# Local attention in a six-layer block on one core: probability transposes moved behind the output product, directly ahead of the next scores

## The chip, the cores and the metric

One core of a Trainium2 chip. The metric is the device time of one execution in microseconds; lower is better. Engines: TensorE (PE) with its weight loads (PEld), VectorE (DVE), ScalarE (ACT), GpSimd (POOL), and SyncE (SP), which issues DMAs.

## The reference, cut to what matters

Input is `x`, (2, 1024, 128), f32. A first small attention with 16 heads of 8 columns and two layer norms comes first, and a layer norm last. In between stand six layers, which take most of the time:

```python
for i in range(6):
    x = attn_layer(shift_tokens(x), Wqkv[i], q_scale[i], k_scale[i], Wo[i]) + x
    x = ffn_layer(shift_tokens(x), ln_g[i], ln_b[i], W1[i], b1[i], W2[i], b2[i]) + x

# attn_layer: 16 heads of 64, windows of 32
q, k, v = split(x @ Wqkv)
q, k = l2norm(q) * qs, l2norm(k) * ksc
q, k = rotary(q), rotary(k)                      # cos, sin and a scale per position
attn = softmax(mask(q @ k.T * 8))                # each row sees itself and the 32 keys before it
out  = (attn @ v) @ Wo
```

`shift_tokens` moves the upper half of the columns by one row.

## The kernel before, in words

It is written in Bass, with a program for each engine and hand-placed semaphores: each engine runs its own list in order, and waits on counters that the others raise. Rows come in 16 tiles of 128. In a layer, `layer` on each engine runs `tiles(...)`, which calls `tile(t, n, p, opening, closing)` for each of the 16 tiles (first and last two written out, the others in a loop of two; `opening` is the first, `closing` the last), and then the feed-forward part in four groups of four tiles. The order of work around the change is thus the order of calls in the `tile` of each engine.

A tile is software-pipelined. While the scores and products of tile t run, the projections of tile t+1 are made, and what is left of tile t-1 is finished:

- `project(t+1, ., x)`, x = 0 to 5 (L1180 to L1182): six blocks of 512 columns of q, k and v in two PSUM banks, three matmuls each. Blocks 0, 1, 2, 4 are q and k, blocks 3 and 5 are v.
- ScalarE: `square` (L494) of a q or k block, `values` (L501) evacuates a v block.
- VectorE: `rotary(t+1, ., j)`, j = 0 to 3: norms (L791, `n` is `n2`), `tc_` (L794), `n2c` (L798), `ts_` (two of L801). It waits for the square.
- GpSimd: `rotate`: a power (L317), a sum (L319), a product into `w_nat` (L322); four times a tile.
- TensorE: `transpose_heads(., j, at)` (L1187) of `w_nat`; ScalarE: `heads_T` (L516) evacuates it to `qT` or `kT`.
- TensorE: `scores(t, n, p, G)`, G = 0 and 1, eight heads each: mask (L1137) and scores (L1146) into the two banks SB.
- VectorE: `maxima(t, p, G)`, two reductions (L748). ScalarE: `exps(t, p, G, b)`, b = 0 and 1, four exponentials each (L478).
- TensorE: `transpose_probs(t, G, b, at)` (L1153). ScalarE: `probs_out` (L487) evacuates to `pT`.
- TensorE: `weigh_values(t, p, G)` (L1166), probabilities by values. VectorE: `heads_out(t, p, G)`, reciprocal (L756) and product into `o_nat` (L758).
- TensorE: `transpose_out(t, G, at)` (L1193). ScalarE: `heads_out_T` (L507) to `oT`. TensorE: `project_out(t, G)` (L1201) with `Wo`. VectorE: `residual` (L765, L766) adds the input.
- `copy_prev` (VectorE, L773) carries the last 32 keys into the next tile; `copy_input` (ScalarE, L426, L427) and `input_rest` (VectorE, L780) prepare the input of tile t+2 in two parts.

The transposes share a ring of two PSUM banks, bank 4 and bank 6, which the last argument of each call (`at`) names. Each use waits until the bank's last content is evacuated; the counters `tp_free` (heads), `pt_evac` (probabilities) and `ot_evac` (outputs) tell that. So whoever moves a transpose also changes what its neighbours wait for. In the last tile of a layer the layer norm of the feed-forward part is interleaved: `transpose_in`, `norm_stats`, `norm`, `transpose_normed`, `normed_T`.

In the order before, the two `transpose_probs` of a group stand three or four steps behind its scores, with two projections, a transpose of heads and a product with the values in between.

Of the kernel before, what the change touches and what calls it, by code (L numbers as in the profile page):

```python
# [6 lines left out]
TILES = B * N // P  # L7
# [38 lines left out]
def build(nc, x, Wa, ba, Wp, bp, Wqkv, Wo, scales, W1, W2, par, rope, ident, identb, mask, mask_l, select, out):  # L46
# [3 lines left out]
    with ctx:  # L50
# [351 lines left out]
        def _(eng):  # L402
# [167 lines left out]
            def layer(l, last):  # L570
                t0 = l * TILES

                def tile(t, n, p, opening, closing):
                    if closing:
                        shifted(l, 0)
                        shifted(l, 1)
                    exps(t, p, 0, 0)
                    if not closing:
                        square(t + 1, 0)
                    heads_T(t, p, 2, 6 if opening else 4)  # L580
                    exps(t, p, 0, 1)
                    if not closing:
                        square(t + 1, 1)
                    probs_out(t, 0, 0, 4 if opening else 6)
                    probs_out(t, 0, 1, 6 if opening else 4)
                    if not opening:
                        heads_out_T(t - 1, 1, 6)
                    if not closing:
                        square(t + 1, 2)
                    heads_T(t, p, 3, 4)  # L590
                    exps(t, p, 1, 0)
                    if closing:
                        normed_T(0)
                    else:
                        values(t + 1, 1 - p, 0)
                        heads_T(t + 1, 1 - p, 0, 6)
                    exps(t, p, 1, 1)
                    if not closing and not (isinstance(n, int) and n == TILES - 2):
                        copy_input(n + 2, p)
                    probs_out(t, 1, 0, 4)  # L600
                    probs_out(t, 1, 1, 6)
                    if not closing:
                        square(t + 1, 3)
                    heads_out_T(t, 0, 4)
                    if closing:
                        normed_T(1)
                    else:
                        values(t + 1, 1 - p, 1)
                        heads_T(t + 1, 1 - p, 1, 6)

# [63 lines left out]
        def _(eng):  # L674
# [202 lines left out]
            def layer(l, last):  # L877
# [45 lines left out]
                def tile(t, n, p, opening, closing):  # L923
# [7 lines left out]
                    if closing:  # L931
                        norm(0)
                    else:
                        rotary(t + 1, n + 1, 1)
                    if not opening:
                        residual(t - 1, n - 1)
                    if closing:
                        norm_stats(1)
                    else:
                        copy_prev(t + 1, n + 1, 1 - p)  # L940
                    maxima(t, p, 1)
                    if closing:
                        norm(1)
                    else:
                        rotary(t + 1, n + 1, 2)
                    heads_out(t, p, 0)
                    if not closing:
                        if not (isinstance(n, int) and n == TILES - 2):
                            input_rest(t + 2, n + 2, p)
                        rotary(t + 1, n + 1, 3)  # L950
# [62 lines left out]
        def _(eng):  # L1013
# [230 lines left out]
            def layer(l, last):  # L1244
# [42 lines left out]
                def tile(t, n, p, opening, closing):  # L1287
# [6 lines left out]
                    else:  # L1294
                        project(t + 1, 1 - p, 0)
                    if opening:
                        eng.wait_ge(tp_free, t * 4 + 1)
                    else:
                        eng.wait_ge(ot_evac, t * 2 - 1)
# [5 lines left out]
                    if not opening:  # L1305
                        weigh_values(t - 1, 1 - p, 1)
                    eng.wait_ge(tp_free, t * 4 + 2)
                    transpose_probs(t, 0, 0, 4 if opening else 6)
                    eng.wait_ge(tp_free, t * 4 + 3)
                    transpose_probs(t, 0, 1, 6 if opening else 4)  # L1310
                    if not opening:
                        eng.wait_ge(pt_evac, t * 4 + 1)
# [3 lines left out]
                    eng.wait_ge(pt_evac, t * 4 + (1 if opening else 2))  # L1316
                    transpose_heads(t, 3, 4)
                    if not opening:
                        project_out(t - 1, 1)
                    scores(t, n, p, 1)  # L1320
                    if not closing:
                        project(t + 1, 1 - p, 3)
                    if opening:
                        eng.wait_ge(pt_evac, t * 4 + 2)
                    else:
                        eng.wait_ge(ot_evac, t * 2)
# [4 lines left out]
                    weigh_values(t, p, 0)  # L1331
                    eng.wait_ge(tp_free, t * 4 + 4)
                    transpose_probs(t, 1, 0, 4)
                    if closing:
                        eng.wait_ge(f_xnT, l * SUPERS + 1)
                    else:
                        eng.wait_ge(tp_free, t * 4 + 5)
                    transpose_probs(t, 1, 1, 6)
                    if not closing:
                        project(t + 1, 1 - p, 4)  # L1340
                    eng.wait_ge(pt_evac, t * 4 + 3)
                    transpose_out(t, 0, 4)
                    if not closing:
                        project(t + 1, 1 - p, 5)
                    eng.wait_ge(pt_evac, t * 4 + 4)
                    if closing:
                        transpose_normed(1)
                    else:
                        transpose_heads(t + 1, 1, 6)
                    project_out(t, 0)  # L1350

                def close_layer(t, n, p):
                    gate_up(0, 0)
                    weigh_values(t, p, 1)
                    eng.wait_ge(ot_evac, t * 2 + 1)
# [101 lines left out]
```

## Time and profile before

| what | value |
|---|---|
| median of 3 runs | 2512.28 us (2510.72 to 2596.46) |
| profiled execution | 2513.5 us, its span 2511.7 us |
| TensorE busy in the span | 2084.1 us |
| VectorE, ScalarE, GpSimd busy | 1743.5, 1632.6, 1740.9 us |
| mean granted TensorE clock | 0.966 of full |

The span is that of the profile's own records; the profiled execution's time is 1.8 us above it. "Idle before" in brackets is the time that an engine stood still right before an instruction, with the one that ended it. PE busy counts matmuls with their pipelined ends. In a timeline, instructions of one line that follow each other are one row, and its second column runs to the end of the last.

### The profile page before, as it was taken

How to read it: one execution, taken by the hardware profiler on the slowest of the kernel's cores; microseconds unless marked ns; L12 is line 12 of the kernel's file. 1: busy time of each engine (PE TensorE's matmuls, PEld its weight loads, DVE VectorE, ACT ScalarE, POOL GpSimd, SP SyncE). 2: the span in 40 equal slices, each digit the busy share in tenths (PEclk: the TensorE clock that was granted, in tenths of full speed). 3: DMA queues.
4: the chain of work that ended last, by engine and by line, in shares of the span. 5: the costliest groups of instructions: out<-in, count | busy, mean ns of one | idle time of the engine just before them, and what ended most of it. 6: DMA issues, size and time to landing. Idle time of an engine off the chain costs nothing.

```text
span 2511.7 us, 70965 instructions
## 1 busy us (share of the span) xinstructions
PE 2084.1 (83%) x23552; PEld 1533.5 (61%) x23552; DVE 1743.5 (69%) x4197; ACT 1632.6 (65%) x5654; POOL 1740.9 (69%) x1364
## 2 busy tenths in 40 slices
PE   6999478888888888888888888888788888888886
PEld 4666356666566666466666466665466665566663
DVE  4555667777667777577776777775777776777764
ACT  3555257767567777577776577776577775777772
POOL 4333468888578787588885788885788885888860
PEclk9999779999999999999999999999999999999998
DMA  1000111111021111111111121111211110111110
GB/s 61 1 0 0 43 53 49 40 38 38 22 75 40 46 40 39 53 45 38 38 48 33 54 50 40 38 39 34 63 41 47 39 38 22 48 44 44 38 37 17
DMA packets 40902, 98.65 MB, mean 39 GB/s; under 512 B 6480, under 2 KB 20432, under 8 KB 39856
## 3 DMA queue, kind: packets, MB, share of 16 engines
q1 hardware_dynamic: 40752, 96.75, 14.9%
q8 instruction: 82, 1.34, 0.2%
q14 instruction: 68, 0.56, 0.1%
HBM read 20.32 MB, written 1.05 MB: 9 GB/s over the span
## 4 chain that ended last, share of the span: by engine, by line
PE 39%; issue 19%; DVE 17%; ACT 15%; POOL 8%; DVEq 1%; POOLq 0%; ACTq 0%; DMA 0%; SPq 0%
ACT prob L478 10%; PE bank L1201 5%; PE bank L1146 5%; DVE nmax L748 3%; PE bank L1193 3%; PE bank L1187 3%; DVE ts_ L801 3%; PE bank L1137 3%; DVE o_nat L758 2%; PE bank L1180 2%; ACT qT L516 2%; POOL tsum L319 2%; PE bank L1182 2%; PE bank L1181 2%; PE bank L1050 2%
## 5 line engine op out<-in xcount | busy, mean ns | idle before, releaser
L317 POOL TENSOR_TENSOR rn<-n2c,half_neg 128x8 f32<-128x8 f32 x384 | 632.9, 1648 | 351.0 <-DVE n2c L798 341.8
L478 ACT ACTIVATE prob<-bank,nmax 128x96 f32<-128x96 f32 x1536 | 508.7, 360 | 401.9 <-DVE nmax L748 401.7
L319 POOL TENSOR_TENSOR tsum<-tc_,ts_ 128x512 f32<-128x512 f32 x384 | 493.3, 1285 | 0.0
L1153 PE MATMUL bank<-idf,prob 128*96 128x128 f32 x1536 | 247.2, 285 | 241.6 <-ACT prob L478 241.6
L322 POOL TENSOR_TENSOR w_nat<-tsum,rn 128x512 f32<-128x512 f32 x384 | 401.0, 1044 | 37.8 <-POOL tsum L319 15.1
L791 DVE TENSOR_REDUCE n<-nat 128x8 f32<-128x512 f32 x384 | 261.3, 680 | 188.9 <-ACT nat L494 122.3
L478 ACT ACTIVATION_READ_ACCUMULATOR prob<-bank,nmax 128x1 f32 x1536 | 347.0, 226 | 0.0
L1153 PEld LDWEIGHTS bank<-idf,prob 128*96 128x96 f32 x1536 | 152.9, 128 | 301.1 <-issue 288.6
L1180 PE MATMUL bank<-w_hi,xs 128*128 128x512 f32 x576 | 288.9, 502 | 9.5 <-DVE ts_ L801 7.0
L801 DVE TENSOR_TENSOR ts_<-bank,ropeL 128x256 f32<-128x256 f32 x768 | 285.8, 412 | 0.0
L748 DVE TENSOR_REDUCE nmax<-bank 128x4 f32<-128x384 f32 x384 | 196.1, 552 | 125.5 <-PE bank L1146 117.6
L494 ACT ACTIVATE nat<-bank 128x512 f32<-128x512 f32 x384 | 235.5, 613 | 55.7 <-PE bank L1182 54.0
L794 DVE TENSOR_TENSOR tc_<-bank,ropeL 128x512 f32<-128x512 f32 x384 | 261.2, 680 | 0.0
L780 DVE TENSOR_TENSOR xs_lo<-xA,xs 64x128 fp32r<-64x128 f32 x192 | 189.0, 984 | 72.7 <-ACT xs L427 69.5
L1187 PE MATMUL bank<-idf,w_nat 128*128 128x128 f32 x1536 | 233.5, 275 | 4.2 <-POOL w_nat L322 2.8
L1182 PE MATMUL bank<-w_hi,xs_lo 128*128 128x512 f32 x576 | 232.5, 404 | 0.5 <-issue 0.5
L1181 PE MATMUL bank<-w_lo,xs 128*128 128x512 f32 x576 | 232.9, 404 | 0.0
L1187 PEld LDWEIGHTS bank<-idf,w_nat 128*128 128x128 f32 x1536 | 192.8, 141 | 62.7 <-issue 6.9
L1166 PEld LDWEIGHTS bank<-vspace,pT 96*64 96x64 f32 x6144 | 195.0, 138 | 52.5 <-issue 52.5
L1166 PE MATMUL bank<-vspace,pT 96*64 96x64 f32 x6144 | 221.5, 225 | 0.0
L487 ACT ACTIVATE pT<-bank 96x512 f32<-96x512 f32 x384 | 213.1, 608 | 11.2 <-PE bank L1153 9.0
L1201 PE MATMUL bank<-oT,wo 128*128 128x128 f32 x1536 | 209.1, 280 | 4.1 <-ACT oT L507 4.1
(129 smaller groups left out, 3988.1 us busy)
## 6 DMA issues: line engine op xcount, KB each, us to landing
vspace<-v_nat SPq DMA_DIRECT2D x96, 384.0 KB, 4.0
vspace<-v_nat SPq DMA_DIRECT2D x96, 256.0 KB, 3.5
vspace<-v_nat SPq DMA_DIRECT2D x95, 128.0 KB, 2.3
nat<-w_qkv SPq DMA_DIRECT2D x5, 1536.0 KB, 7.8
wo<-w_o SPq DMA_DIRECT2D x6, 512.0 KB, 4.0
w<-w SPq DMA_DIRECT2D x6, 341.0 KB, 3.0
shared<-w_qkv SPq DMA_DIRECT2D x1, 1536.0 KB, 6.6
w<-w SPq DMA_DIRECT2D x6, 192.0 KB, 3.0
```

The source lines that it names most:

```text
L317: nc.gpsimd.tensor_tensor(rn[:, r, :], n2c[:, r, :], half_neg[:, 0:8], ALU.pow).then_inc(pool_step, 1)
L319: nc.gpsimd.tensor_tensor(tsum[:, r, :], tc_[:, r, :], ts_[:, r, :], ALU.add).then_inc(pool_step, 1)
L322: nc.gpsimd.tensor_tensor(w_nat[:, r, :].rearrange("p (h d) -> p h d", d=D), tsum[:, r, :].rearrange("p (h d) -> p h d", d=D), rn[:, r, :] ...
L478: last = nc.scalar.activation(prob[:, 4 * b + i, :], SB[b][:, i * SPAN:(i + 1) * SPAN], ACT.Exp, bias=nmax[:, p, 8 * G + 4 * b + i:8 * G + ...
L801: last = nc.vector.tensor_tensor(ts_[:, r, :].rearrange(heads3, d=D)[:, :, lo:lo + D // 2], pj[:, :].rearrange(heads3, d=D)[:, :, hi:hi + ...
L1153: last = nc.tensor.transpose(RING[at][0:SPAN, i * P:(i + 1) * P], prob[:, 4 * b + i, :], idf[:, :])
L1166: last = nc.tensor.matmul(OB[qs, a:a + D], pT[:, 4 * b + i, qs], vw[:, p, half, head * D:(head + 1) * D], start=True, stop=True, skip_grou ...
L1180: nc.tensor.matmul(PJ[x % 2][:, :], xs[:, p, :], hi, start=True, stop=False)
L1181: nc.tensor.matmul(PJ[x % 2][:, :], xs[:, p, :], rest, start=False, stop=False)
L1182: nc.tensor.matmul(PJ[x % 2][:, :], xs_lo[:, p, :], hi, start=False, stop=True).then_inc(pj_ready, 1)
L1187: last = nc.tensor.transpose(RING[at][:, i * P:(i + 1) * P], w_nat[:, j % 2, i * P:(i + 1) * P], idf[:, :])
L1201: last = nc.tensor.matmul(YB[:, 0:P], wo[:, 4 * G + i, :], oT[:, G, i * P:(i + 1) * P], start=G == 0 and i == 0, stop=G == 1 and i == 3)
```

## The change

Three engines' lists are reordered; no arithmetic is added or taken away, and SyncE and GpSimd are untouched. On TensorE, `weigh_values` of the group before moves up to directly behind the first projection; the two `transpose_probs` of a group move down behind `project_out`, directly ahead of the next group's scores; the bank numbers and waits are changed to fit. ScalarE follows: the second `exps` comes before the copy of heads, and `probs_out` goes to where its transposes now are. On VectorE, `residual` and `copy_prev` move from ahead of the second maxima to behind `rotary(., 2)` and `heads_out`.

```diff
 # ScalarE, tile
                     exps(t, p, 0, 0)
                     if not closing:
                         square(t + 1, 0)
+                    exps(t, p, 0, 1)
                     heads_T(t, p, 2, 6 if opening else 4)
-                    exps(t, p, 0, 1)
                     if not closing:
                         square(t + 1, 1)
-                    probs_out(t, 0, 0, 4 if opening else 6)
-                    probs_out(t, 0, 1, 6 if opening else 4)
                     if not opening:
                         heads_out_T(t - 1, 1, 6)
                     if not closing:
                         square(t + 1, 2)
                     heads_T(t, p, 3, 4)
+                    probs_out(t, 0, 0, 6)
+                    probs_out(t, 0, 1, 4)
                     exps(t, p, 1, 0)
...
                         values(t + 1, 1 - p, 0)
+                    exps(t, p, 1, 1)
+                    if not closing:
                         heads_T(t + 1, 1 - p, 0, 6)
-                    exps(t, p, 1, 1)
...
                         heads_T(t + 1, 1 - p, 1, 6)
+                    probs_out(t, 1, 0, 4)
+                    probs_out(t, 1, 1, 6)
 # VectorE, tile
                     if closing:
                         norm(0)
+                        norm_stats(1)
                     else:
                         rotary(t + 1, n + 1, 1)
-                    if not opening:
-                        residual(t - 1, n - 1)
-                    if closing:
-                        norm_stats(1)
-                    else:
-                        copy_prev(t + 1, n + 1, 1 - p)
                     maxima(t, p, 1)
                     if closing:
                         norm(1)
                     else:
                         rotary(t + 1, n + 1, 2)
+                    if not opening:
+                        residual(t - 1, n - 1)
                     heads_out(t, p, 0)
                     if not closing:
+                        copy_prev(t + 1, n + 1, 1 - p)
                         if not (isinstance(n, int) and n == TILES - 2):
                             input_rest(t + 2, n + 2, p)
                         rotary(t + 1, n + 1, 3)
 # TensorE, tile
                         project(t + 1, 1 - p, 0)
+                    if not opening:
+                        weigh_values(t - 1, 1 - p, 1)
                     if opening:
                         eng.wait_ge(tp_free, t * 4 + 1)
                     else:
-                        eng.wait_ge(ot_evac, t * 2 - 1)
+                        eng.wait_ge(pt_evac, t * 4 - 1)
                     transpose_heads(t, 2, 6 if opening else 4)
...
                         project(t + 1, 1 - p, 1)
                     if not opening:
-                        weigh_values(t - 1, 1 - p, 1)
-                    eng.wait_ge(tp_free, t * 4 + 2)
-                    transpose_probs(t, 0, 0, 4 if opening else 6)
-                    eng.wait_ge(tp_free, t * 4 + 3)
-                    transpose_probs(t, 0, 1, 6 if opening else 4)
-                    if not opening:
-                        eng.wait_ge(pt_evac, t * 4 + 1)
+                        eng.wait_ge(pt_evac, t * 4)
                         transpose_out(t - 1, 1, 6)
                     if not closing:
                         project(t + 1, 1 - p, 2)
-                    eng.wait_ge(pt_evac, t * 4 + (1 if opening else 2))
+                    eng.wait_ge(tp_free, t * 4 + (2 if opening else 3))
                     transpose_heads(t, 3, 4)
                     if not opening:
                         project_out(t - 1, 1)
+                    if opening:
+                        eng.wait_ge(tp_free, t * 4 + 3)
+                    else:
+                        eng.wait_ge(ot_evac, t * 2)
+                    transpose_probs(t, 0, 0, 6)
+                    eng.wait_ge(tp_free, t * 4 + 4)
+                    transpose_probs(t, 0, 1, 4)
+
                     scores(t, n, p, 1)
                     if not closing:
                         project(t + 1, 1 - p, 3)
...
+                    weigh_values(t, p, 0)
+                    eng.wait_ge(pt_evac, t * 4 + 1)
                     if closing:
                         transpose_normed(0)
                     else:
                         transpose_heads(t + 1, 0, 6)
-                    weigh_values(t, p, 0)
-                    eng.wait_ge(tp_free, t * 4 + 4)
+                        project(t + 1, 1 - p, 4)
+                    eng.wait_ge(pt_evac, t * 4 + 2)
+                    transpose_out(t, 0, 4)
+                    if closing:
+                        eng.wait_ge(f_xnT, l * SUPERS + 1)
+                        transpose_normed(1)
+                    else:
+                        project(t + 1, 1 - p, 5)
+                        eng.wait_ge(tp_free, t * 4 + 5)
+                        transpose_heads(t + 1, 1, 6)
+                    project_out(t, 0)
+                    eng.wait_ge(ot_evac, t * 2 + 1)
                     transpose_probs(t, 1, 0, 4)
...
                     transpose_probs(t, 1, 1, 6)
-                    if not closing:
-                        project(t + 1, 1 - p, 4)
-                    eng.wait_ge(pt_evac, t * 4 + 3)
-                    transpose_out(t, 0, 4)
...
-                    project_out(t, 0)
```

The instruction lists show the same. On TensorE, in the half tile between scores(t, ., ., 0) and scores(t, ., ., 1) of a layer's second tile, behind the scores and project 0, the kernel before has:

```order
L1187 MATMUL bank<-idf,w_nat 128x128 x4
L1180 MATMUL bank<-w_hi,xs 128x512
L1181 MATMUL bank<-w_lo,xs 128x512
L1182 MATMUL bank<-w_hi,xs_lo 128x512
L1166 MATMUL bank<-vspace,pT 64x64 x16
L1153 MATMUL bank<-idf,prob 96x128 x8
L1193 MATMUL bank<-idf,o_nat 128x128 x4
L1180 MATMUL bank<-w_hi,xs 128x512
L1181 MATMUL bank<-w_lo,xs 128x512
L1182 MATMUL bank<-w_hi,xs_lo 128x512
L1187 MATMUL bank<-idf,w_nat 128x128 x4
L1201 MATMUL bank<-oT,wo 128x128 x4
```

In the changed kernel (its TensorE lines are two lower, so L1151 is the probability transpose) TensorE has at the same place:

```order
L1164 MATMUL bank<-vspace,pT 64x64 x16
L1185 MATMUL bank<-idf,w_nat 128x128 x4
L1178 MATMUL bank<-w_hi,xs 128x512
L1179 MATMUL bank<-w_lo,xs 128x512
L1180 MATMUL bank<-w_hi,xs_lo 128x512
L1191 MATMUL bank<-idf,o_nat 128x128 x4
L1178 MATMUL bank<-w_hi,xs 128x512
L1179 MATMUL bank<-w_lo,xs 128x512
L1180 MATMUL bank<-w_hi,xs_lo 128x512
L1185 MATMUL bank<-idf,w_nat 128x128 x4
L1199 MATMUL bank<-oT,wo 128x128 x4
L1151 MATMUL bank<-idf,prob 96x128 x8
```

The product with the values went from behind the second projection to ahead of the heads' transposes, and the eight probability transposes from ahead of the output transposes to the end of the half. On VectorE, in a layer's third tile, the kernel before has between rotary(., 1) and the end of heads_out(t, 0):

```order
L765 TENSOR_TENSOR xB<-bank,xA 128x1
L766 TENSOR_TENSOR xB<-bank,xA 128x128
L773 TENSOR_SCALAR kT<-kT,follows 128x8x32
L748 TENSOR_REDUCE nmax<-bank 128x4 x2
L791 TENSOR_REDUCE n<-nat 128x8
L794 TENSOR_TENSOR tc_<-bank,ropeL 128x512
L798 TENSOR_SCALAR n2c<-n 128x8
L801 TENSOR_TENSOR ts_<-bank,ropeL 128x8x32 x2
L756 RECIPROCAL linv<-lsum 128x8
L758 TENSOR_TENSOR o_nat<-bank,linv 128x512
```

and the changed kernel:

```order
L748 TENSOR_REDUCE nmax<-bank 128x4 x2
L791 TENSOR_REDUCE n<-nat 128x8
L794 TENSOR_TENSOR tc_<-bank,ropeL 128x512
L798 TENSOR_SCALAR n2c<-n 128x8
L801 TENSOR_TENSOR ts_<-bank,ropeL 128x8x32 x2
L765 TENSOR_TENSOR xB<-bank,xA 128x1
L766 TENSOR_TENSOR xB<-bank,xA 128x128
L756 RECIPROCAL linv<-lsum 128x8
L758 TENSOR_TENSOR o_nat<-bank,linv 128x512
L773 TENSOR_SCALAR kT<-kT,follows 128x8x32
```

The residual (L765, L766) now stands between the rotary and heads_out, and the copy of keys (L773) behind heads_out.

## Rows read from the trace of the kernel before

**Rows 1.** The page: busy time of each engine, TensorE's slices, one group
```profile
PE 2084.1 (83%) x23552; PEld 1533.5 (61%) x23552; DVE 1743.5 (69%) x4197; ACT 1632.6 (65%) x5654; POOL 1740.9 (69%) x1364
...
PE   6999478888888888888888888888788888888886
...
L780 DVE TENSOR_TENSOR xs_lo<-xA,xs 64x128 fp32r<-64x128 f32 x192 | 189.0, 984 | 72.7 <-ACT xs L427 69.5
```

**Rows 2.** Stretch of six tiles: us; PE, PEld, DVE, ACT, POOL busy; clock; DMA
```profile
865.09:980.70 115.61, 97.98 (x1237) 76.56 (x1237) 89.02 (x198) 84.68 (x300) 94.45 (x74) 1.00 0.17 41
```

**Rows 3.** Waits in the same six tiles: total us, times, longest
```profile
POOL rn L317 <- DVE n2c L798: 18.2, 12, 1.6
...
PE bank L1153 <- ACT prob L478: 13.8, 12, 1.5
```

**Rows 4.** Timeline, half A: start us, us, engine, line, [idle before <- releaser]
```profile
913.37 0.50 PE L1137 MATMUL bank<-mskL,idb 128*128 x2
...
914.76 1.02 DVE L748 TENSOR_REDUCE nmax<-bank 128x4 f32<-128x384 f32 x2 [0.77 <-PE bank L1146]
...
916.63 0.61 ACT L494 ACTIVATE nat<-bank 128x512 f32<-128x512 f32 x1
...
917.38 0.69 DVE L791 TENSOR_REDUCE n<-nat 128x8 f32<-128x512 f32 x1 [1.60 <-ACT nat L494]
...
917.73 0.64 PE L1153 MATMUL bank<-idf,prob 128*96 128x128 f32 x4
...
919.16 0.61 PE L1153 MATMUL bank<-idf,prob 128*96 128x128 f32 x4 [0.79 <-ACT prob L478]
919.32 0.19 DVE L756 RECIPROCAL linv<-lsum 128x8 f32<-128x8 f32 x1
...
920.29 0.66 PE L1193 MATMUL bank<-idf,o_nat 128*128 128x128 f32 x4 [0.51 <-DVE o_nat L758]
...
922.91 0.50 PE L1137 MATMUL bank<-mskL,idb 128*128 x2
```

**Rows 5.** Timeline, half B of the tile before it
```profile
903.66 0.50 PE L1137 MATMUL bank<-mskL,idb 128*128 x2
904.00 0.16 DVE L765 TENSOR_TENSOR xB<-bank,xA 128x1 f32 x1 [0.84 <-PE bank L1201]
...
904.41 0.35 DVE L773 TENSOR_SCALAR kT<-kT,follows 128x256 f32<-128x256 f32 x1
...
905.98 0.67 DVE L791 TENSOR_REDUCE n<-nat 128x8 f32<-128x512 f32 x1
...
909.45 0.61 PE L1153 MATMUL bank<-idf,prob 128*96 128x128 f32 x4 [1.48 <-ACT prob L478]
...
909.82 0.48 PE L1180 MATMUL bank<-w_hi,xs 128*128 128x512 f32 x1
```

**Rows 6.** Stretches: first and last of the 7 half tiles with a fallen clock
```profile
366.18:377.58 11.40, 9.69 (x106) 7.72 (x104) 8.84 (x19) 7.54 (x26) 9.24 (x8) 0.85 0.01 1
...
2383.61:2394.93 11.32, 9.69 (x105) 7.78 (x104) 8.84 (x19) 7.60 (x26) 8.93 (x8) 0.85 0.00 0
```

**Rows 7.** Stretches behind the last probability transposes of layers 1, 2 and 6
```profile
644.20:647.80 3.60, 3.35 (x21) 2.25 (x19) 0.00 (x0) 3.21 (x5) 0.00 (x0) 1.00 0.00 0
1006.80:1010.40 3.60, 3.54 (x19) 3.14 (x18) 0.00 (x0) 2.72 (x4) 0.00 (x0) 0.54 0.00 0
...
2447.70:2451.30 3.60, 3.60 (x19) 3.23 (x18) 0.00 (x0) 2.57 (x4) 0.00 (x0) 0.55 0.00 0
```

**Rows 8.** Timelines: last tile of layer 2, first tile of layer 3
```profile
1000.45 0.16 DVE L765 TENSOR_TENSOR xB<-bank,xA 128x1 f32<-128x1 f32 x1 [2.20 <-PE bank L1201]
...
1004.37 0.61 PE L1153 MATMUL bank<-idf,prob 128*96 128x128 f32 x4 [1.14 <-ACT prob L478]
...
1006.33 0.62 PE L1153 MATMUL bank<-idf,prob 128*96 128x128 f32 x4 [1.35 <-ACT prob L478]
...
1065.51 1.06 PE L1153 MATMUL bank<-idf,prob 128*96 128x128 f32 x4 [3.60 <-ACT prob L478]
```

More of the change, by code:

```diff
@@ L595, in tile @@
                         values(t + 1, 1 - p, 0)
+                    exps(t, p, 1, 1)
+                    if not closing:
                         heads_T(t + 1, 1 - p, 0, 6)
-                    exps(t, p, 1, 1)
[L598 to L601, printed above, removed]
-                    if not closing:
+                        if not (isinstance(n, int) and n == TILES - 2):
+                            copy_input(n + 2, p)
                         square(t + 1, 3)
@@ L1322, in tile @@
                         project(t + 1, 1 - p, 3)
[L1323 to L1326, printed above, removed]
+                    weigh_values(t, p, 0)
+                    eng.wait_ge(pt_evac, t * 4 + 1)
                     if closing:
@@ L1330, in tile @@
                         transpose_heads(t + 1, 0, 6)
-                    weigh_values(t, p, 0)
-                    eng.wait_ge(tp_free, t * 4 + 4)
+                        project(t + 1, 1 - p, 4)
[10 more added lines that the diff above has]
+                    eng.wait_ge(ot_evac, t * 2 + 1)
                     transpose_probs(t, 1, 0, 4)
                     if closing:
-                        eng.wait_ge(f_xnT, l * SUPERS + 1)
+                        eng.wait_ge(f_xnT, l * SUPERS + 2)
                     else:
-                        eng.wait_ge(tp_free, t * 4 + 5)
+                        eng.wait_ge(tp_free, t * 4 + 6)
                     transpose_probs(t, 1, 1, 6)
-                    if not closing:
-                        project(t + 1, 1 - p, 4)
-                    eng.wait_ge(pt_evac, t * 4 + 3)
-                    transpose_out(t, 0, 4)
[L1343 to L1349, printed above, removed]
-                    project_out(t, 0)
                 def close_layer(t, n, p):
@@ L1354, in close_layer @@
                     weigh_values(t, p, 1)
-                    eng.wait_ge(ot_evac, t * 2 + 1)
+                    eng.wait_ge(pt_evac, t * 4 + 3)
                     transpose_out(t, 1, 4)
```

## The prediction

> **What bounds the kernel now.** Start with the page. Its busy shares put TensorE at 83% and no other engine above 69% [rows 1]; the 40 slices look alike from the sixth to the last but one, so one repeating piece carries the time. That piece is the attention tile. I looked next at the table of stretches, for six tiles in the middle of layer 2: 115.61 us, or 19.27 per tile, at full clock; TensorE is busy 97.98 of it (16.3 per tile), GpSimd 94.45 (15.7) [rows 2]. No engine is full: about 2.9 us of TensorE per tile are waits, and a tile could not go far under 16.4. The list of waits of the same stretch names them: TensorE before the probability transposes waits 13.8 us in 12 waits for the exponentials; GpSimd waits 18.2 us for `n2c` [rows 3]. So the tile is a loop of dependences that goes through all engines. The two timelines show it. I call the part from scores(t,0) to scores(t,1) half A (it takes 922.91 - 913.37 = 9.54 us [rows 4]) and the part from scores(t,1) to the next tile's scores half B (913.37 - 903.66 = 9.71 [rows 4, 5]).
>
> In half A the path from the scores is: maxima 1.39 us after the scores start, the exponentials, the square of projection 0 at 3.26, VectorE's rotary(0) from 4.01, the reciprocal of heads_out(t-1,1) at 5.95, and the transposes of that output at 6.92, for which TensorE stands still 0.51 us although it also did the probability transposes meanwhile (from 4.36 and from 5.79, after a wait of 0.79) [rows 4]. 2.62 us later the next scores start [rows 4]. In half B the path is scores, maxima, both blocks of exponentials; TensorE waits 1.48 us for the second, and goes on at 5.79 [rows 5].
>
> **The change, part by part.** It adds and removes no arithmetic instruction; it moves some.
>
> (1) *Half A, first part.* The chain scores, maxima, first exponentials, square, rotary(0), heads_out is the same on ScalarE and VectorE in the new order. weigh_values(t-1,1) moves ahead of the transposes of heads 2, and ends early, but VectorE takes heads_out only behind rotary(0), whose square stands behind the first four exponentials. So the output transposes still cannot start before 6.92 us after the scores. What stood in front of them is gone, though: the two blocks of probability transposes now come later. TensorE's remaining work there (scores, project 0, weigh, heads 2, project 1) is what stands in the first 4.36 us of the old half A [rows 4]; so TensorE now idles from about 4.5 to 6.9 us, 2.4 us in one piece, where it had 0.79 and 0.51 in two.
>
> (2) *Half A, second part.* Behind the output transposes come project 2, heads 3, project_out as before (2.62 us to where the scores stood), and now the two blocks of probability transposes, on the path: one block holds TensorE 909.82 - 909.45 = 0.37 us [rows 5], two 0.74. The exponentials are long done, so there is no wait. Half A: 6.92 + 2.62 + 0.74 = 10.28, against 9.54: +0.74.
>
> (3) *Half B.* The probability transposes at its middle are gone, and with them the 1.48 us wait. What is late next is VectorE. In the new order it goes maxima, rotary(2), residual, heads_out(t,0). From the scores to the first instruction of the rotary is 905.98 - 903.66 = 2.32 us [rows 5]; a rotary takes 919.32 - 917.38 = 1.94 us [rows 4]; the residual, moved to this place, 904.41 - 904.00 = 0.41 [rows 5]; from the reciprocal to the output transposes 920.29 - 919.32 = 0.97 [rows 4]. Together 5.64. TensorE has less work than that in front of them (project 3, weigh, heads 0, project 4), so it waits here too, though under 1 us at a time. Then 2.62 + 0.74 = 3.36 as in half A. Half B: 9.00, against 9.71: -0.71.
>
> (4) *The tile.* 10.28 + 9.00 = 19.28, against 19.25. The order by itself gives nothing: the waits for the exponentials are exchanged for waits for heads_out, and the transposes leave the shade of a wait for the path. The sum contains no small gaps; I take +0.1 per tile, bounds -0.1 to +0.4 (the upper one if the copy of keys and the remainder of the input, now behind heads_out on VectorE, push rotary(3) into the next maxima: they took 0.35 us [rows 5] and 2 x 0.98 [rows 1], and there is 3.36 + 1.39 = 4.75 us for them and the rotary's 1.94, so about 0.5 spare). For 84 tiles (14 inner ones in each of 6 layers) that is +8 us, bounds -8 to +34.
>
> (5) *TensorE's clock.* This is what I expect to decide. The trace shows how idle stretches and the granted clock go together. With a single idle stretch of 1.48 us per tile the clock stays at full (2.4 GHz) nearly always: the six tiles above have a granted clock of 1.00 [rows 2]. In 7 half tiles of the whole run it fell to half (1.2 GHz) right behind that wait, mean 0.85 over the half tile; the first and the last of them took 11.40 and 11.32 us where 9.71 is usual: +1.65 [rows 5, 6]. In the last tile of a layer TensorE idles twice within 3 us, 1.14 and 1.35 [rows 8], and behind it the clock is 0.54 in layer 2 and falls like that in five of the six layers (not in the first) [rows 7]. In a layer's first tile an idle stretch of 3.60 us ends with four transposes that take 1.06 us in place of 0.61: half clock [rows 8]. So: 1.5 us, rarely (7 of 84); 2.5 us in two pieces, 5 of 6; 3.6 us, yes. The new 2.4 us stretch in every tile sits next to the second. I take two tiles in three, bounds none and all. What follows the stretch at half clock (output transposes, project 2, heads 3, project_out, probability transposes) is all on the path, so each fall costs its full 1.65 us: 84 x 2/3 x 1.65 = +92 us, bounds 0 and +139. The 7 old falls, 7 x 1.65 = 12 us, come off.
>
> The Trainium skill (TensorE: Matmul & The Clock Gate, section "Why this matters for your kernels") speaks of the same danger but asks only that TensorE-idle gaps between bursts stay below a length that is above my 2.4 us. By that rule no clock would fall here, and the time would be that of the first rival below. The trace disagrees with it as it stands: the clock fell behind waits of 1.48 us.
>
> (6) *Edges of a layer.* First tile: the two blocks of probability transposes used to stand in front of a wait for heads 3 and now follow it: +0.74 x 6 = +4. Last tile: VectorE's residual waited 2.20 us for project_out with the second norm statistics and the maxima queued behind it [rows 8]; they now go ahead of it. I take -1.5 per layer (0 to -2.2 by that row, and something back because transpose_normed(1) now stands ahead of the last probability transposes): -9. Together -5, bounds -12 to +6. SyncE's and GpSimd's orders are untouched; the values' DMA is issued after the same signals, half a tile and more before it is used.
>
> *The sum:* profiled execution 2513.5 (span 2511.7) + 8 + 92 - 12 - 5 = 2596.5; the median of the runs, 2512.3, lies 1.2 below that execution, so 2595.
>
> **The rivals.**
> *A. The clock stands.* The order acts as in (1) to (4) but the 2.4 us stretch does not trip the clock: 2513.5 + 8 - 5 - 1 = 2516 (the old falls kept; without them 2504). For it: the first layer's last tile kept its clock [rows 7], and 77 of 84 waits of 1.5 us did. Against it: the five others.
> *B. Faster: the waits vanish.* If VectorE had heads_out ready when project 1 is done, half A would keep only the +0.74 less its old waits, and half B lose its 1.48: about 19.27 - 1.48 = 17.8 per tile, 84 x -1.48 = -124: 2388. It decides at 4.5 us after the scores; the row has the reciprocal at 5.95 and the transposes at 6.92 [rows 4], and nothing on VectorE's or ScalarE's way there is taken out. At the extreme, all 2.9 us of waits gone, GpSimd (15.7) and TensorE (16.3) would bound the tile.
> *C. VectorE late as well.* The copy of keys and the input remainder are held by GpSimd's additions, rotary(3) ends after the next scores, and the maxima wait: +0.4 per tile on top of falls in nearly every tile: 2513.5 + 34 + 139 - 12 - 5 - 1 = 2668.
>
> **How the numbers follow.** Forecast case 0.65, A 0.23, B 0.04, C 0.08. The forecast case runs from 2558 (two falls in five tiles) to 2642 (a fall in every tile); with A below it the range is 2510 to 2640, which leaves out B, most of C and little else. About 2% (2462 and 2562.5) is what a measurement of this kernel can tell from no change. Slower by more: the forecast case and C, less the low end of the first: 0.70. Within: 0.26. Faster: 0.04.
>
> **What would show it.** In the changed profile: per inner tile, output transposes of heads_out 6.9 us after the first scores behind an idle stretch of about 2.4 us released by `o_nat`; no wait of L1151 (the probability transposes) for the exponentials; half A at 10.3 (11.9 where the clock falls), half B at 9.0; a mean granted clock of about 0.90 to 0.93 in the middle of a layer, where it was 1.00; GpSimd's waits for `n2c` not shorter. I am wrong on (1) if the output transposes come before 6 us; on (5) if the middle of a layer keeps a clock of 1.00; on (3) if TensorE doesn't wait for `o_nat` in half B; on (4) if tiles at full clock take under 18.9 or over 19.7.

## The result and the profile after

The changed kernel takes 2611.9 us (median of 4 runs, 2608.3 to 2698.8), the kernel before beside it 2513.0 (2510.7 to 2596.5). The ratio is 1.038, with a 95% interval of 1.032 to 1.044: slower. (One run of each, the highest, was disturbed and is left out of the ratio.) The forecast was 2595 with a range of 2510 to 2640. The profiled execution took 2608.3 us, its span is 2606.4, its mean granted clock 0.936 (0.966 before).

The page of the changed kernel: busy times (one line) and three groups (line, engine, shapes, count | busy us, mean ns | idle before, releaser). They answer to [rows 1]:

```profile
PE 2165.5 (83%) x23552; PEld 1599.1 (61%) x23552; DVE 1729.8 (66%) x4197; ACT 1645.9 (63%) x5654; POOL 1747.3 (67%) x1364
...
L478 ACT ACTIVATE prob<-bank,nmax 128x96 f32<-128x96 f32 x1536 | 506.7, 355 | 211.5 <-DVE nmax L748 211.3
...
L1178 PE MATMUL bank<-w_hi,xs 128*128 128x512 f32 x576 | 299.9, 521 | 83.1 <-DVE ts_ L801 80.7
L1191 PE MATMUL bank<-idf,o_nat 128*128 128x128 f32 x768 | 147.8, 324 | 235.6 <-DVE o_nat L758 225.1
```

The busy share reads 83% again, and tells nothing: TensorE did the same 23552 matmuls in 81 us more of busy time. The probability transposes no longer wait; the output transposes (L1191) wait 225 us for `o_nat`, and projections 81 us for `ts_`. The page of the kernel before has instead:

```profile
L1153 PE MATMUL bank<-idf,prob 128*96 128x128 f32 x1536 | 247.2, 285 | 241.6 <-ACT prob L478 241.6
```

The timeline of a half A at full clock, in the middle of layer 3, answers to [rows 4] (start us, us, engine, line, [idle before <- releaser]):

```profile
1209.07 0.49 PE L1135 MATMUL bank<-mskL,idb 128*128 x2
...
1210.45 1.02 DVE L748 TENSOR_REDUCE nmax<-bank 128x4 f32<-128x384 f32 x2 [0.43 <-PE bank L1144]
...
1213.15 0.69 DVE L791 TENSOR_REDUCE n<-nat 128x8 f32<-128x512 f32 x1 [1.68 <-ACT nat L494]
...
1215.08 0.19 DVE L756 RECIPROCAL linv<-lsum 128x8 f32<-128x8 f32 x1
...
1216.06 0.66 PE L1191 MATMUL bank<-idf,o_nat 128*128 128x128 f32 x4 [2.41 <-DVE o_nat L758]
...
1218.57 1.04 PE L1151 MATMUL bank<-idf,prob 128*96 128x128 f32 x8
...
1219.44 0.49 PE L1135 MATMUL bank<-mskL,idb 128*128 x2
```

The reciprocal starts 6.01 us after the scores and the output transposes 6.99; before, it was 5.95 and 6.92. TensorE idles 2.41 us in one piece. The eight probability transposes stand at the end, with no wait, and half A is 10.37 us. In the next tile the same half meets half clock. First its rows in the timeline of TensorE, then stretches (us; PE, PEld, DVE, ACT, POOL busy; clock; DMA): the half A above (with the 0.12 us before it), the half B behind it, and this half A.

```profile
1235.51 0.99 PE L1191 MATMUL bank<-idf,o_nat 128*128 128x128 f32 x4 [2.33 <-DVE o_nat L758]
1236.15 0.78 PE L1178 MATMUL bank<-w_hi,xs 128*128 128x512 f32 x1
...
1239.65 1.04 PE L1151 MATMUL bank<-idf,prob 128*96 128x128 f32 x8
```

```profile
1208.95:1219.44 10.49, 8.08 (x106) 6.45 (x105) 7.09 (x18) 7.04 (x25) 8.62 (x7) 1.00 0.29 72
1219.44:1228.60 9.16, 8.51 (x105) 6.44 (x103) 7.69 (x16) 7.28 (x27) 7.23 (x6) 1.00 0.03 7
1228.60:1240.52 11.92, 9.59 (x105) 7.79 (x103) 6.94 (x18) 7.03 (x25) 10.26 (x8) 0.86 0.25 61
```

Behind the 2.33 us the four transposes take 0.99 instead of 0.66 and a projection's first matmul 0.78 instead of 0.48: the granted clock is 0.86 over this half, where it is 1.00 in the other two, so for a part of it the clock was at its lower level of 1.2 GHz. This half takes 11.92.

Half B of the same tile answers to [rows 5]:

```profile
1221.76 0.68 DVE L791 TENSOR_REDUCE n<-nat 128x8 f32<-128x512 f32 x1
...
1223.68 0.15 DVE L765 TENSOR_TENSOR xB<-bank,xA 128x1 f32 x1
...
1223.82 0.51 PE L1178 MATMUL bank<-w_hi,xs 128*128 128x512 f32 x1 [0.50 <-DVE ts_ L801]
1223.94 0.19 DVE L756 RECIPROCAL linv<-lsum 128x8 f32<-128x8 f32 x1
...
1224.17 0.69 DVE L758 TENSOR_TENSOR o_nat<-bank,linv 128x512 f32<-128x512 f32 x1
...
1224.39 0.39 PE L1180 MATMUL bank<-w_hi,xs_lo 128*128 128x512 f32 x1
...
1224.91 0.66 PE L1191 MATMUL bank<-idf,o_nat 128*128 128x128 f32 x4
...
1226.09 0.59 ACT L507 ACTIVATE oT<-bank 128x512 f32<-128x512 f32 x1
...
1226.73 1.16 PE L1199 MATMUL bank<-oT,wo 128*128 128x128 f32 x8
```

The rotary begins at 2.32 after the scores, projection 4 waits 0.50 for it, the output transposes come at 5.47 and project_out at 7.29.

Counting the distances between the starts of the mask matmuls over the 14 inner tiles of each of the six layers gives the account of the inner tiles, in the one profiled execution of each kernel. "Falls" are half tiles of 10.8 us or more; in every kernel these are the same half tiles as those in which the granted clock was under 1.00, and the medians leave them out. The longest wait is that of an inner tile between 1110 and 1340 us.

| kernel | half A, median | half B, median | falls in 84 tiles | mean tile | longest TensorE wait in a tile | run median |
|---|---|---|---|---|---|---|
| before | 9.54 | 9.72 | 7 (B) | 19.39 | 1.5 | 2513.0 |
| changed | 10.32 | 9.16 | 54 (A) | 20.44 | 2.4 | 2611.9 |
| fill6 | 10.32 | 9.15 | 0 | 19.51 | 1.0 | 2529.9 |
| fill2 | 10.32 | 9.15 | 44 (A) | 20.32 | 2.0 | 2599.7 |
| resback | 10.37 | 9.16 | 57 (A) | 20.48 | 2.4 | 2609.8 |
| resci | 10.39 | 8.75 | 63 (A) | 20.44 | 2.4, in most tiles 2.1 | 2607.3 |
| hofirst | 9.28 | 9.66 | 21 (B) | 19.33 | 1.3 | 2512.6 |
| hoffill | 9.29 | 9.67 | 0 | 18.95 | 0.4 | 2477.0 |
| hyb | 9.53 | 9.23 | 0 | 18.79 | 1.0 | 2466.8 |
| hybresci | 9.60 | 9.12 | 0 | 18.84 | 1.0 | 2466.7 |

The rows from fill6 on are the experiments told below. The changed kernel's inner tiles are 84 x (20.44 - 19.39) = 88 us longer in sum than those before. The spans differ by 2606.4 - 2511.7 = 94.7.

### The profile page after: what moved, and what is told of

Read it like the earlier page. It is cut to its first block, busy times and chain, and to the rows that moved or that the text cites. A ratio compares the mean times of both kernels' runs of the same rounds, so it can differ in the third digit from the quotient of the medians.

```text
span 2606.4 us, 71177 instructions
## 1 busy us (share of the span) xinstructions
PE 2165.5 (83%) x23552; PEld 1599.1 (61%) x23552; DVE 1729.8 (66%) x4197; ACT 1645.9 (63%) x5654; POOL 1747.3 (67%) x1364
## 3 DMA queue, kind: packets, MB, share of 16 engines
HBM read 20.32 MB, written 1.05 MB: 8 GB/s over the span
## 4 chain that ended last, share of the span: by engine, by line
PE 47%; DVE 22%; issue 15%; ACT 7%; POOL 7%; DVEq 1%; POOLq 0%; ACTq 0%; DMA 0%; SPq 0%
PE bank L1199 7%; PE bank L1151 6%; PE bank L1144 5%; PE bank L1191 4%; DVE ts_ L801 4%; ACT prob L478 4%; DVE o_nat L758 4%; DVE nmax L748 4%; PE bank L1185 3%; DVE n L791 3%; PE bank L1135 2%; PE bank L1178 2%; ACT nat L494 2%; PE bank L1048 2%; PE bank L1180 2%
## 5 line engine op out<-in xcount | busy, mean ns | idle before, releaser
L322 POOL TENSOR_TENSOR w_nat<-tsum,rn 128x512 f32<-128x512 f32 x384 | 410.6, 1069 | 37.8 <-POOL tsum L319 15.1
L1178 PE MATMUL bank<-w_hi,xs 128*128 128x512 f32 x576 | 299.9, 521 | 83.1 <-DVE ts_ L801 80.7
L1191 PE MATMUL bank<-idf,o_nat 128*128 128x128 f32 x768 | 147.8, 324 | 235.6 <-DVE o_nat L758 225.1
L478 ACT ACTIVATION_READ_ACCUMULATOR prob<-bank,nmax 128x1 f32 x1536 | 339.0, 221 | 0.0
L1191 PEld LDWEIGHTS bank<-idf,o_nat 128*128 128x128 f32 x768 | 94.0, 158 | 313.3 <-DVE o_nat L758 285.0
L1185 PE MATMUL bank<-idf,w_nat 128*128 128x128 f32 x1536 | 266.4, 301 | 6.9 <-ACT qT L516 4.1
L1180 PE MATMUL bank<-w_hi,xs_lo 128*128 128x512 f32 x576 | 242.2, 420 | 0.0
L1179 PE MATMUL bank<-w_lo,xs 128*128 128x512 f32 x576 | 241.4, 419 | 0.4 <-issue 0.4
L1199 PE MATMUL bank<-oT,wo 128*128 128x128 f32 x1536 | 226.9, 294 | 8.7 <-ACT oT L507 6.9
L1199 PEld LDWEIGHTS bank<-oT,wo 128*128 128x128 f32 x1536 | 203.6, 206 | 31.9 <-ACT oT L507 31.4
```

What stands on the lines that cost most here:

```text
L322: nc.gpsimd.tensor_tensor(w_nat[:, r, :].rearrange("p (h d) -> p h d", d=D), tsum[:, r, :].rearrange("p (h d) -> p h d", d=D), rn[:, r, :] ...
L478: last = nc.scalar.activation(prob[:, 4 * b + i, :], SB[b][:, i * SPAN:(i + 1) * SPAN], ACT.Exp, bias=nmax[:, p, 8 * G + 4 * b + i:8 * G + ...
L1178: nc.tensor.matmul(PJ[x % 2][:, :], xs[:, p, :], hi, start=True, stop=False)
L1185: last = nc.tensor.transpose(RING[at][:, i * P:(i + 1) * P], w_nat[:, j % 2, i * P:(i + 1) * P], idf[:, :])
L1191: last = nc.tensor.transpose(RING[at][:, i * P:(i + 1) * P], o_nat[:, G, i * P:(i + 1) * P], idf[:, :])
L1199: last = nc.tensor.matmul(YB[:, 0:P], wo[:, 4 * G + i, :], oT[:, G, i * P:(i + 1) * P], start=G == 0 and i == 0, stop=G == 1 and i == 3)
```

## The experiments

**Filler in the idle stretch.** Is it the clock, or do the waits cost the time and the clock only goes along? The changed kernel gets matmuls into bank 6, whose results the output transposes overwrite:

```diff
                         eng.wait_ge(pt_evac, t * 4)
+                        if not closing:
+                            for _ in range(6):
+                                nc.tensor.matmul(RING[6][:, :], xs[:, 1 - p, :], w_hi[:, 0:HB], start=True, stop=True)
                         transpose_out(t - 1, 1, 6)
```

> The changed kernel with six matmuls of 128x512 (projection operands, results thrown away) issued into bank 6 just ahead of transpose_out(t-1, 1, 6), where TensorE idles 2.4 us; some 1.4 us of work, hidden if it all fits. Clock theory: idle stretch down to about 1 us, the clock stays at full in the middle of a layer (1.00), every half A takes 10.3, none 11.8; 84 x 2/3 x 1.6 = 90 us less: about 2520. Rival, the order of waits alone costs the time and the clock only goes along with it: no change, 2612, half A still between 10.3 and 12. If the filler is in the way: over 2612.

> As fill6 with two matmuls: idle stretch about 1.9 us. Clock theory: fewer falls than the two tiles in three of the changed kernel, more than with six; 2530 to 2590, each fall still 1.6 us in its half A. Rival: 2612.

Measured: six fillers 2529.9 us, two 2599.7, which is above the 2530 to 2590 that I expected; the ratios to the kernel before are 1.007 (1.005 to 1.010) and 1.035 (1.030 to 1.040), where the change alone has 1.038. The stretch 1110 to 1340 us (middle of layer 3) of the kernel before, the changed one, fill6 and fill2, one line each, from the table of stretches (clock third from the end):

```profile
1110.00:1340.00 230.00, 194.60 (x2466) 151.89 (x2465) 176.71 (x394) 168.69 (x599) 187.63 (x144) 1.00 0.17 41
```

```profile
1110.00:1340.00 230.00, 194.42 (x2273) 152.13 (x2274) 164.05 (x371) 158.76 (x557) 176.50 (x134) 0.94 0.16 38
```

```profile
1110.00:1340.00 230.00, 210.90 (x2515) 163.60 (x2508) 172.94 (x391) 167.63 (x596) 185.66 (x142) 1.00 0.17 41
```

```profile
1110.00:1340.00 230.00, 201.85 (x2312) 158.68 (x2311) 161.95 (x367) 158.66 (x555) 178.17 (x136) 0.94 0.16 38
```

And TensorE's waits for `o_nat` in the same stretch (total us, times, longest), changed, fill6, fill2:

```profile
PE bank L1191 <- DVE o_nat L758: 28.5, 12, 2.4
```

```profile
PE bank L1191 <- DVE o_nat L758: 11.0, 11, 1.0
```

```profile
PE bank L1191 <- DVE o_nat L758: 21.1, 11, 2.0
```

More work on TensorE makes the kernel some 80 us faster (82 by the medians, (1.038 - 1.007) x 2510 = 78 by the ratios). The chain that TensorE waits for is no shorter (half A at full clock stays 10.32 in all three); what differs is that TensorE idles less of that time, and the clock. That settles the rival: the falls cost some 80 us of the 99, and all else, the order and the edges less the old falls, the remaining 0.7%. With the wait down to 2.0 us the falls go only from 54 to 44.

**VectorE's residual and copy of keys back ahead of the second maxima.** This was a term of my sum for half B.

```diff
+                    if not opening:
+                        residual(t - 1, n - 1)
+                    if not closing:
+                        copy_prev(t + 1, n + 1, 1 - p)
                     maxima(t, p, 1)
...
-                    if not opening:
-                        residual(t - 1, n - 1)
                     heads_out(t, p, 0)
                     if not closing:
-                        copy_prev(t + 1, n + 1, 1 - p)
```

> The changed kernel with VectorE's residual and copy_prev back ahead of the second maxima, where VectorE idles 2.9 us. My step (3): the residual's 0.41 us leaves the path of half B, 9.16 becomes 8.75 to 8.8, 84 x -0.4 = -34: about 2578. Rival, half B is bound by the wait of project 4 for ts_ and by ScalarE, not by heads_out: half B stays at 9.1, 2612.

Measured: 2609.8, ratio 1.039 (1.034 to 1.044): no gain, so the rival of this expectation holds, and half B is 9.16 as in the changed kernel. A half B of it, from the scores at 1218.94:

```profile
1223.32 0.51 PE L1179 MATMUL bank<-w_hi,xs 128*128 128x512 f32 x1 [0.50 <-DVE ts_ L801]
...
1224.15 0.66 PE L1192 MATMUL bank<-idf,o_nat 128*128 128x128 f32 x4
...
1226.23 1.16 PE L1200 MATMUL bank<-oT,wo 128*128 128x128 f32 x8 [0.28 <-ACT oT L507]
```

The output transposes come at 5.21 us after the scores (5.23 is what my sum without the residual gives), 0.26 earlier than in the changed kernel, and 0.26 is what the residual takes there (1223.68 to the reciprocal at 1223.94). But project_out waits for ScalarE's `oT` and still starts at 7.29. ScalarE's list (four exponentials, values, four exponentials, heads, two input copies, square, then `oT`) ends at the same time with either order of VectorE: `oT` starts 6.65 us after the scores in both.

**ScalarE's input copies moved behind `oT`, on top of that.**

```diff
-                        if not (isinstance(n, int) and n == TILES - 2):
-                            copy_input(n + 2, p)
                         square(t + 1, 3)
                     heads_out_T(t, 0, 4)
+                    if not closing and not (isinstance(n, int) and n == TILES - 2):
+                        copy_input(n + 2, p)
```

> As resback, and ScalarE's copy_input moved behind heads_out_T(t, 0) and square 3. In resback the output transposes came 0.26 us earlier but project_out then waited 0.28 for oT, which ScalarE copies last in its list. If ScalarE's list is what holds half B: project_out at 6.8 in place of 7.3 us after the scores, half B 8.7 in place of 9.16, time 2610 - 84 x 0.45 = 2572; two tiles in three still with a fallen clock. Rival, half B is bound elsewhere (projection 4's wait for ts_): half B stays 9.1, 2610. If the late input remainder on VectorE pushes rotary 3 into the next maxima: half A grows by what half B loses.

Half B did what the ScalarE account says, the time did not follow: half B 8.75, but 2607.3 us where 2572 was expected, ratio 1.039 (1.036 to 1.041). In a half B from the scores at 1216.81 to those at 1225.55:

```profile
1222.79 0.63 ACT L507 ACTIVATE oT<-bank 128x512 f32<-128x512 f32 x1
...
1223.64 1.06 PE L1200 MATMUL bank<-oT,wo 128*128 128x128 f32 x8
...
1227.02 1.01 DVE L748 TENSOR_REDUCE nmax<-bank 128x4 f32<-128x384 f32 x2
```

`oT` starts at 5.98 and project_out at 6.83 (6.8 expected). So ScalarE's list did hold half B, once the residual was out of the way; its copies were not moved alone. What became of 84 x 0.4 = 34 us: the late input remainder pushes rotary(3) into the next maxima, which start 1.47 us after their scores instead of 1.38 (half A 10.39 instead of 10.32, 6 us); half B's mean is 8.89, not its median of 8.75 (12 us more); and the clock fell in 63 tiles instead of 54 (9 x 1.5 = 14 us). These are read off, not tested one by one. The idle stretch of half A also looks different here: in 53 of the 84 tiles it is 2.0 to 2.2 us with another of some 0.3 us ahead of it, and the clock fell in 40 of them; in the other 31 it is 2.4 us, with 23 falls. So 2.1 us behind 0.3 is followed by a fall as often (75%) as 2.4 us in one piece (74%).

**heads_out ahead of rotary on VectorE.** Step (1) says that the 2.4 us exist because heads_out(t-1, 1) stands behind rotary(t+1, 0).

```diff
                     maxima(t, p, 0)
+                    if not opening:
+                        heads_out(t - 1, 1 - p, 1)
                     if closing:
                         norm_stats(0)
                     else:
                         rotary(t + 1, n + 1, 0)
-                    if not opening:
-                        heads_out(t - 1, 1 - p, 1)
```

> The changed kernel with VectorE's heads_out(t-1, 1) ahead of rotary(t+1, 0). My step (1): the output transposes start at about 4.4 us after the scores in place of 6.9; then project 2 waits for ts_ of rotary 0 until about 6.2; idle stretch about 1.5; half A about 9.2 in place of 10.3 / 11.9, clock nearly always full: 84 x -1.1 - 90 = -182: about 2430, faster than both. Rival, the second half of the chain (exponentials, squares on ScalarE) holds half A: half A stays over 10 and the time over 2500.

Measured: 2512.6, ratio 1.002 (0.999 to 1.005): 99 us better than the changed kernel, but no better than the one before, and far from the 2430 that I expected. Half A is 9.28 and without a fall, as expected. Half B grew from 9.16 to 9.66, and 21 tiles have a fall in it. The timeline of such a half B, from the scores at 1200.52:

```profile
1203.90 1.04 POOL L322 TENSOR_TENSOR w_nat<-tsum,rn 128x512 f32<-128x512 f32 x1
1204.03 0.94 DVE L798 TENSOR_SCALAR n2c<-n 128x8 f32<-128x8 f32 x1
...
1204.89 0.74 DVE L801 TENSOR_TENSOR ts_<-bank,ropeL 128x256 f32<-128x256 f32 x2
...
1205.68 0.50 PE L1178 MATMUL bank<-w_hi,xs 128*128 128x512 f32 x1 [1.28 <-DVE ts_ L801]
```

VectorE's `n2c`, eight numbers a row, takes 0.94 us instead of 0.16: it started 0.13 us into GpSimd's 1.04 us product and ended 0.03 behind it. `ts_` and projection 4 are late by that, and TensorE idles 1.28 us. My expectation had no such term. That the product holds `n2c` is read from the times; no run moves the one away from the other and leaves the rest.

**hofirst with filler** in both halves (four matmuls ahead of each wait):

```diff
                         eng.wait_ge(pt_evac, t * 4)
+                        if not closing:
+                            for _ in range(4):
+                                nc.tensor.matmul(RING[6][:, :], xs[:, 1 - p, :], w_hi[:, 0:HB], start=True, stop=True)
                         transpose_out(t - 1, 1, 6)
...
                         transpose_heads(t + 1, 0, 6)
+                        for _ in range(4):
+                            nc.tensor.matmul(RING[4][:, :], xs[:, 1 - p, :], w_hi[:, 0:HB], start=True, stop=True)
                         project(t + 1, 1 - p, 4)
```

> As hofirst, with four filler matmuls of 128x512 ahead of the output transposes of half A (bank 6) and four ahead of project 4 in half B (bank 4), about 1 us each. hofirst had half A 9.27, half B 9.66 and 22 half tiles with a fallen clock, idle stretches of 1.28 and 1.23 us. Clock theory: no falls, 2512 - 22 x 1.6 = 2477. Rival, falls come from the whole tile's mix and not from its idle stretches, or the filler is in the way: 2510 or more.

Measured 2477.0, ratio 0.986 (0.983 to 0.989); halves 9.29 and 9.67, no falls. The gain over hofirst is 35 us by the medians and 39 by the ratios; the 21 falls of the inner tiles at 1.6 us each are 34 of it.

**Half A as before, half B as changed.** The change joins a half that loses 0.8 us with a half that wins 0.55. This is hyb. On TensorE, for the ring of banks (ScalarE's first half follows its old order):

```diff
-                    if not opening:
-                        weigh_values(t - 1, 1 - p, 1)
...
                         project(t + 1, 1 - p, 1)
                     if not opening:
+                        weigh_values(t - 1, 1 - p, 1)
+                    if opening:
+                        eng.wait_ge(tp_free, t * 4 + 2)
+                    else:
                         eng.wait_ge(pt_evac, t * 4)
+                    transpose_probs(t, 0, 0, 4 if opening else 6)
+                    eng.wait_ge(tp_free, t * 4 + 3)
+                    transpose_probs(t, 0, 1, 6 if opening else 4)
...
-                    transpose_probs(t, 0, 0, 6)
-                    eng.wait_ge(tp_free, t * 4 + 4)
-                    transpose_probs(t, 0, 1, 4)
                     scores(t, n, p, 1)
...
                     weigh_values(t, p, 0)
-                    eng.wait_ge(pt_evac, t * 4 + 1)
+                    if opening:
+                        eng.wait_ge(pt_evac, t * 4 + 2)
+                    else:
+                        eng.wait_ge(ot_evac, t * 2)
```

> Half A in the order before (probability transposes of group 0 in the middle), half B in the changed order, with the waits on the ring's banks to fit. My account: half A 9.5 to 9.6 with idle stretches of 0.8 and 0.5, half B 9.16; 18.7 per tile against 19.25, few falls of the clock (under 15): 84 x -0.55 - 10 = -56: about 2455, faster than both. Rival 1, the short half B only exists because half A does its work: tile 19.2, time 2510. Rival 2, a shorter tile makes GpSimd's sums hold VectorE's n2c as in hofirst: half B 9.6, 2490.

hybresci adds to hyb what resci has: VectorE's residual and copy of keys ahead of the second maxima, and ScalarE's input copies behind `oT`.

> hyb with both moves of resci. If each does what is claimed: half A 9.55, half B 8.7, 18.25 per tile: 2513 - 84 x 1.0 - 10 = 2420. If VectorE and GpSimd get in each other's way as the tile shortens (GpSimd needs 15.8 to 16.0): 18.7 and 2455, no better than hyb.

Measured: hyb 2466.8, ratio 0.982 (0.980 to 0.985), 1.8% faster than the kernel before (2455 was expected) and 145 us under the changed one; hybresci 2466.7, ratio 0.983 (0.980 to 0.985), no better (2420 was expected, 2455 by its rival). In hyb, over the same 230 us of the middle, the clock is full and no wait of TensorE is over 1.0 us (stretch, then waits):

```profile
1110.00:1340.00 230.00, 201.38 (x2554) 155.79 (x2552) 180.57 (x412) 172.44 (x610) 189.33 (x145) 1.00 0.17 41
```

```profile
POOL rn L317 <- DVE n2c L798: 27.3, 23, 1.6
PE bank L1178 <- DVE ts_ L801: 10.2, 12, 0.9
PE bank L1151 <- ACT prob L478: 9.6, 12, 1.0
...
PE bank L1191 <- DVE o_nat L758: 5.7, 11, 0.5
```

Half A is 9.53 and half B 9.23, 0.07 more than in the changed kernel: the short half B stands by itself, so rival 1 falls. Rival 2 came in part: TensorE waits 0.85 us for `ts_` in half B where it waited 0.50, since `n2c` takes 0.52 us beside GpSimd's product, but most of that doesn't reach the next scores. hybresci shows that at 18.8 us per tile ScalarE's list is no longer what holds: by the medians half A grew by 0.07 and half B won 0.11, but the mean of half B is 9.24 against 9.23 and the mean tile is no shorter. What holds it then was not tested.

## Why the prediction was right, and where it was off

(1) *The chain to heads_out holds half A.* Right: the output transposes come 6.99 us after the scores (6.92 forecast), behind 2.41 us of idling (2.4). hofirst shows it by taking the cause away: half A falls by 1.04.

(2) *Probability transposes on the path, +0.74.* Half A went from 9.54 to 10.32: +0.78. Right.

(3) *Half B, 9.00 from VectorE's list.* It is 9.16, and the sum came that close because two errors nearly cancel. The output transposes came at 5.47, not 5.64: the chain rotary, residual, heads_out holds them as I said (`o_nat` ends at 1224.86, they start at 1224.91), but the residual takes 0.26 us in its new place, not 0.41. Behind them come 3.69 us, not 3.36, because project_out waits for ScalarE's `oT`. resback takes the residual away and the transposes come 0.26 earlier, with no gain; resci moves ScalarE's copies too, and project_out starts 0.46 earlier. I had set as a sign of being wrong here that TensorE does not wait for `o_nat` in half B. That sign came out nearly in full: projection 4, itself 0.50 us late for `ts_`, ends at 1224.78, so that at most 0.13 us of such a wait is left, and none of the 12 waits in the list above is a half B's. The failed step: I summed one chain and left ScalarE's row of copies behind the second exponentials out.

(4) *The order by itself, +8 us with bounds -8 to +34.* The tile at full clock is 10.32 + 9.16 = 19.48 against 9.54 + 9.72 = 19.26, so 84 x 0.22 = +18. Right within its bounds, the size off by half. The mechanism of rival C is there, its price is not. The copy of keys is held in the changed kernel, but VectorE has the time for it: the next maxima still wait for TensorE (same half B as above).

```profile
1224.78 1.46 DVE L773 TENSOR_SCALAR kT<-kT,follows 128x256 f32<-128x256 f32 x1
1224.80 1.28 POOL L319 TENSOR_TENSOR tsum<-tc_,ts_ 128x512 f32<-128x512 f32 x1
...
1229.98 1.02 DVE L748 TENSOR_REDUCE nmax<-bank 128x4 f32<-128x384 f32 x2 [0.44 <-PE bank L1144]
```

It takes 1.46 us beside GpSimd's sum, where it took 0.35 in [rows 5].

(5) *The clock decides.* Right: the chief term. I took two tiles in three at 1.65 us, +92, less 12 for the old falls; it was 54 of 84 (64%) at (11.30 - 10.32) x 84 / 54 = 1.52 us, +82, and fill6 won back 82. Rival A is refuted: with idle stretches of 2.0 and 2.4 us the clock fell in 44 to 63 of 84 tiles. The rule of the Trainium skill (TensorE: Matmul & The Clock Gate, section "Why this matters for your kernels") would let a gap of 2.4 us pass, and does not hold for this kernel. The share itself was an interpolation between three rows, and two thirds had luck in it. The granted clock in the middle of layer 3 was 0.94, where I had given 0.90 to 0.93 as the sign.

(6) *Edges of a layer, -5.* Wrong in sign, and outside the bounds of -12 to +6. Over the six layers the first tiles are 0.3 us shorter (+4 forecast), the first halves of the last tiles 3.1 longer, and what follows up to the next layer's scores 6.6 longer (-9 forecast for the last tiles): +9. The part in front of the first layer, which the change doesn't touch, took 3 us less in this execution. The first half of a layer's last tile takes 8.93 instead of 8.35, and in its second half TensorE idles for `o_nat`, since heads_out stands behind the second norm:

```profile
1024.63 0.66 PE L1257 MATMUL bank<-idf,xn 128*128 128x128 f32 x4
1027.91 1.12 PE L1191 MATMUL bank<-idf,o_nat 128*128 128x128 f32 x4 [2.63 <-DVE o_nat L758]
```

I had seen only what the residual's wait gives back. This was read, not tried.

Together: forecast +8 + 92 - 12 - 5 = +83; read from the traces +18 + 82 - 11 + 9 = +98, less the 3 us in front of the first layer, where the spans differ by 95 and the medians by 99. The 15 us between the two sums are +10 from (4), -10 and +1 from (5), +14 from (6).

## What to carry to other kernels

When a product is moved into the shade of another wait, follow the wait that it used to shade: here the exponentials' wait went, and the one for the normalised output, which had been hidden behind the same transposes, came out whole. Look at how long each idle piece of TensorE is, and not only at their sum: nearly the same 2.8 to 2.9 us of idling per tile cost some 70 us more in pieces of 2.4 and 0.5 than in pieces of 1.5, 0.8 and 0.5 (82 less the 11 of the old falls). And take a symmetric reordering half by half: one half of this one was good and the other bad, and only the joint result was slower.

## What was not expected of the hardware

- The clock against the longest idle stretch of a tile, over 84 tiles each: 0.4 and 1.0 us, no falls (hoffill, fill6, hyb, hybresci); 1.3, 21 falls; 1.5, 7; 2.0, 44; 2.4, 54 and 57; 2.1 or 2.4, 63 (resci). It is not the length alone: hofirst idles 1.24 us in half A and 1.28 in half B, and all 21 falls are in half B. And within the changed kernel the waits that a fall follows (2.33 to 2.49 us) are about as long as those that none follows (2.31 to 2.42). What else decides was not tested.
- A fall cost 1.5 to 1.6 us of time in each of these kernels, and filler matmuls that compute nothing were a gain: 82 us (fill6), 12 (fill2) and 35 (hoffill).
- A VectorE instruction on 128x8 numbers (`n2c`) takes 0.16 us, but 0.94 where GpSimd's 1.04 us product had just begun. Of hofirst's 384, 186 start during such a product or GpSimd's sum and take 0.95 in the median, most of them ending 0.03 us behind it; the other 198 take 0.16. This fits the 0.5 us per tile by which half B is longer in hofirst than in the changed kernel.
